# Leaving two products and the router in PSUM banks: a fused state-space, attention and expert kernel on one core

## The reference, cut to what matters

```python
def _ssm_layer(x, A_log, Dp, W_dbc, W_dt, b_dt):
    A = -jnp.exp(A_log)
    dbc = jnp.einsum('ble,ce->blc', x, W_dbc)
    delta, Bm, Cm = jnp.split(dbc, [DT_RANK, DT_RANK + N_STATE], axis=-1)
    delta = jax.nn.softplus(jnp.einsum('blr,er->ble', delta, W_dt) + b_dt)
    dA = jnp.exp(delta[..., None] * A)
    dBx = (delta * x)[..., None] * Bm[:, :, None, :]
    ...
    _, hs = jax.lax.associative_scan(combine, (dA, dBx), axis=1)
    y = jnp.einsum('blen,bln->ble', hs, Cm)
    return y + Dp * x
...
for i in range(NUM_LAYERS):
    x = _ssm_layer(x, A_log[i], D[i], W_dbc[i], W_dt[i], b_dt[i])
    if i < NUM_LAYERS - 1:
        ...
        x = x[:, :l // 2 * 2].reshape(b, l // 2, 2, d).mean(axis=2)
...
y = A * jnp.einsum('bhni,bhnj,bhije->bhne', qn, qn, kv_mod) + scale ** 2 * Bc * jnp.einsum('bhnd,bhde->bhne', qn, kv) + scale ** 4 * Cc * vsum
...
expert_logits = jax.nn.softmax(rh @ router_w2 + router_b2, axis=-1)
top_w, top_i = jax.lax.top_k(expert_logits, TOP_K)
routing_weights = jax.nn.softmax(top_w, axis=-1)
```

## Time and profile before

| | kernel before |
|---|---|
| runs, median (lowest to highest) | 741.2 us (737.34 to 743.2) |
| the profiled execution's span | 739.2 us |
| TensorE (PE) busy | 649.1 us, 88% |
| VectorE (DVE) busy | 569.2 us, 77% |
| ScalarE (ACT) busy | 519.2 us, 70% |
| GpSimd (POOL) busy | 361.2 us, 49% |
| chain that ended last, by engine | PE 46%, DVE 20%, ACT 14%, DMA 6%, issue 5%, SP queue 4%, POOL 2% |

### The profile page before, as it was taken

One profiled execution on the slowest core, in us unless ns is written; L12 is line 12 of the kernel. 1 busy time (PEld: TensorE's weight loads), 2 busy tenths in 40 slices (PEclk: granted clock), 3 DMA queues, 4 the chain that ended last, 5 costly groups with the idle time before them and its releaser, 6 DMA issues.

```text
span 739.2 us, 25719 instructions
## 1 busy us (share of the span) xinstructions
PE 649.1 (88%) x11131; PEld 375.6 (51%) x11131; DVE 569.2 (77%) x1078; ACT 519.2 (70%) x964; POOL 361.2 (49%) x317
## 2 busy tenths in 40 slices
PE   2667778989998899999989999898999999999983
PEld 2234445555546466545655465554565645555431
DVE  3879789988796799987698779885989986465451
ACT  1244358787868697778858787777887768878762
POOL 7444667757262727485355354472656563221010
PEclk9989899999999999999999999999999999999996
DMA  4332122122102111202112112221110100000001
GB/s 94 67 69 49 38 65 51 45 46 57 44 10 52 28 44 31 62 22 50 44 26 66 29 43 57 61 48 39 34 29 16 25 17 13 19 2 13 13 12 27
DMA packets 77596, 28.72 MB, mean 39 GB/s; under 512 B 69281, under 2 KB 77473, under 8 KB 77473
## 3 DMA queue, kind: packets, MB, share of 16 engines
q1 hardware_dynamic: 71300, 25.92, 15.4%
q10 hardware_dynamic: 6173, 1.05, 0.8%
HBM read 13.25 MB, written 3.05 MB: 22 GB/s over the span
## 4 chain that ended last, share of the span: by engine, by line
PE 46%; DVE 20%; ACT 14%; DMA 6%; issue 5%; SPq 4%; POOL 2%; ACTq 2%; POOLq 0%; DVEq 0%
PE ring L1244 9%; PE ring L1258 7%; PE ring L1346 5%; PE ring L1359 4%; ACT pm L1048 4%; DVE carry_A L1683 3%; PE ring L1425 2%; SPq L726 2%; PE ring L1231 2%; PE ring L1434 2%; PE ring L1211 2%; DVE hidw L1796 2%; DMA x_C<-x_C 1%; DMA x_B<-x_B 1%; PE ring L1454 1%
## 5 line engine op out<-in xcount | busy, mean ns | idle before, releaser
L1048 ACT ACTIVATE pm<-ring,two_col 93x744 f32<-93x744 f32 x128 | 106.6, 874 | 19.1 <-PE ring L1346 18.4
L908 POOL TENSOR_TENSOR q_exp<-qk,mask_q 128x1488 f32<-128x1488 f32 x16 | 44.3, 2771 | 37.1 <-DVE qk L1741 37.0
L1346 PE MATMUL ring<-q_exp,qk 32*93 32x372 f32 x512 | 56.1, 509 | 4.4 <-ACT yT L1055 0.7
L1796 DVE TENSOR_TENSOR hidw<-hid,ring 128x744 f32<-128x744 f32 x48 | 44.3, 923 | 15.7 <-PE ring L1415 8.1
L886 POOL TENSOR_TENSOR du_A<-delta_A,x_A 128x744 f32<-128x744 f32 x16 | 30.0, 1875 | 53.9 <-ACT delta_A L986 39.2
L1083 ACT ACTIVATE hid<-ring,b_col 128x372 f32<-128x372 f32 x96 | 49.3, 568 | 8.3 <-PE ring L1434 4.5
L1359 PE MATMUL ring<-pm,v 97*32 97x93 f32 x2048 | 53.1, 245 | 0.5 <-ACT pm L1048 0.4
L1090 ACT ACTIVATE hid<-ring,b_col 128x744 f32<-128x744 f32 x48 | 42.3, 881 | 15.1 <-PE ring L1425 10.8
L1359 PEld LDWEIGHTS ring<-pm,v 97*32 97x32 f32 x2048 | 42.1, 110 | 14.2 <-issue 4.9
L893 POOL TENSOR_TENSOR base_A<-base_A,carry_A 128x744 f32<-128x744 f32 x16 | 33.2, 2076 | 32.0 <-DVE carry_A L1695 27.9
L919 POOL CAST gate_part<-gate 93x144 bf16<-93x144 f32 x16 | 5.4, 336 | 83.4 <-DVE gate L1791 83.4
(11 more groups left out here) (349 smaller groups left out, 1839.7 us busy)
## 6 DMA issues: line engine op xcount, KB each, us to landing
xin_A<-in_x_dram SPq DMA_DIRECT2D x62, 93.0 KB
xin_B<-in_x_dram SPq DMA_DIRECT2D x62, 93.0 KB
x_A<-x_A SPq DMA_DIRECT2D x32, 93.0 KB, 2.3
x_B<-x_B SPq DMA_DIRECT2D x32, 93.0 KB, 2.9
x_C<-x_C SPq DMA_DIRECT2D x32, 93.0 KB, 2.2
out_dram<-osb SPq DMA_DIRECT2D x15, 186.0 KB
x_D<-x_D SPq DMA_DIRECT2D x32, 46.5 KB, 2.0
w<-in_L_ffn_expert_w_dram SPq DMA_DIRECT2D x6, 48.0 KB
```

The costliest lines, as they stand in the source:

```text
L1048: a.activation(pm[q % 2][h][0:TOUT].rearrange("m a j n -> m a (j n)"), out_of(f"att.s{q}{h}", g)[0:TOUT, :, 0:COLS], ACT.Square, bias=two_ ...
L1346: ins = mm(o[h][0:TOUT, b, 0:COLS], qk[r:r + 32, 1, q * TOUT:(q + 1) * TOUT], q_exp[r:r + 32, q].rearrange("p j n -> p (j n)"), start=True ...
L1796: tt(hidw[k][:], hid2[:], out_of(f"ffn.g_{k}", g)[:, :, 0:COLS], ALU.mult).then_inc(me, 1)
```

## The change

The product b * du is written in place over b in its two PSUM banks, and the scan reads it there, with dec from SBUF; operands and operations change places, so that the state is decay * state + b * du. For that the b job writes 744 neighbouring columns across two banks (the first half starts at column 512 - 372), and state 0 is taken out of the sum in `s` (row 0 of w_c0 is zero). The product s * du is written in place over s, and D * x is added to it from there. The router's four arrays stand in the bank of its logits at columns 0, 64, 128 and 192, one of the one-hot arrays excepted. So b's banks are now freed by `scan`, s's by `based`, the logits' bank by `gate`. The number of VectorE and TensorE steps stays as it is, but for one preparation step (`prep.back`, 13 small VectorE instructions in place of GpSimd's 9 on row_back). The SBUF tiles vin, lg, pr, key and one oh are gone. ORDER is new on every engine, and so are the banks.

```diff
         JOBS = {f"{u}.{j}": (2, f"dve {u}.{r}") for u in UNITS
-                for j, r in (("z", "quad"), ("b", "vin"), ("s", "base"), ("c", "carry"))}
+                for j, r in (("z", "quad"), ("b", "scan"), ("s", "based"), ("c", "carry"))}
...
-                 "ffn.rh": (2, "act ffn.rh"), "ffn.lg": (1, "dve ffn.route1"), "ffn.gT": (1, "act ffn.gateT"),
+                 "ffn.rh": (2, "act ffn.rh"), "ffn.lg": (1, "dve ffn.gate"), "ffn.gT": (1, "act ffn.gateT"),
...
+        def b_made(u, g):
+
+            return out_of(f"{u}.b", g).rearrange("p b c -> p (b c)")[:, 512 - WIDE[u]:512 + WIDE[u]]
+
+        def router(g, k):
+
+            n_at = 64 * ("lg", "pr", "key", "rsum").index(k)
+            o_ = out_of("ffn.lg", g)[0:TOUT, 0]
+            return o_[:, n_at:n_at + GB] if k == "rsum" else o_[:, n_at:n_at + GB * NX].rearrange("m (b e) -> m b e", e=NX)
...
-            spots = sem("spots")
-            for t_ in row_back.values():
-                g.memset(t_[:], 0.0).then_inc(spots, 1)
...
                 if s == "vin":
-                    o = made_by("b")
+                    need(g, f"pe {u}.b")
                     need(g, f"pool {u}.du")
-                    tt(halves(vin[u][:, 1:W + 1]), o, halves(du[u][:]), ALU.mult).then_inc(me, 1)
+                    tt(b_made(u, g), b_made(u, g), du[u][:], ALU.mult).then_inc(me, 1)
                 if s == "scan":
                     need(g, f"dve {u}.vin", f"act {u}.decay")
                     need(g, f"pool {u}.y", back=1)
-                    v.tensor_tensor_scan(carry[u][:], vin[u][:, 0:W], dec[u][:], 0.0, ALU.add, ALU.mult).then_inc(me, 1)
+                    v.tensor_tensor_scan(carry[u][:], dec[u][:], b_made(u, g), 0.0, ALU.mult, ALU.add).then_inc(me, 1)
                 if s == "base":
                     o = made_by("s")
                     need(g, f"pool {u}.du")
-                    need(g, f"pool {u}.{'y' if u == 'D' else 'pooled'}", back=1)
-                    tt(halves(base[u][:]), o, halves(du[u][:]), ALU.mult).then_inc(me, 1)
+                    tt(o, o, halves(du[u][:]), ALU.mult).then_inc(me, 1)
                 if s == "based":
                     need(g, f"dve {u}.base")
-                    stt(halves(base[u][:]), xs[u][:, 0::2, :], d_col[:, l:l + 1], halves(base[u][:]), ALU.mult, ALU.add).then_inc(me, 1)
+                    need(g, f"pool {u}.{'y' if u == 'D' else 'pooled'}", back=1)
+                    stt(halves(base[u][:]), xs[u][:, 0::2, :], d_col[:, l:l + 1], out_of(f"{u}.s", g)[:, :, 0:wide],
+                        ALU.mult, ALU.add).then_inc(me, 1)
```

In the table ORDER the first entries of the lists of act and sp read before and now:

```diff
-            "act": ("prep.l3:0 A.x:0 B.x:0 prep.exp:0 prep.l2:0 prep.l5:0 A.row:0 B.row:0 A.exp:0 A.ln:0 B.exp:0 ...
+            "act": ("prep.l5:0 B.x:0 prep.exp:0 A.x:0 B.row:0 A.row:0 B.exp:0 B.ln:0 A.exp:0 A.ln:0 A.decay:0 ...
-            "sp": ("prep.l4:0 prep.l1:0 A.load:0 B.load:0 A.swap:0 B.swap:0 prep.l0:0 B.load:1 A.load:1 ...
+            "sp": ("A.load:0 B.load:0 prep.l4:0 A.load:1 B.swap:0 A.swap:0 prep.l1:0 B.load:1 prep.l0:0 ...
```

More of the change, by code:

```diff
@@ L1654, in prepare @@
                     dve.wait_ge(c, 14)
-                k = ("w0", "w1", "w2", "dec", "mean", "qkvp", "late", "cen", "most", "mostof", "ends", "flags", "again").index(s)
+                k = ("w0", "w1", "w2", "dec", "mean", "qkvp", "late", "cen", "most", "mostof", "ends", "flags", "again", "back").index(s)
                 v.memset(tick[:, k:k + 1], 0.0).then_inc(me, 1)
@@ L1778, in experts @@
[L1778 to L1783 removed]
+                    step(v.tensor_reduce(st[:, 1], pr, AX_X, ALU.add), "sum")
```

103 lines of the change are left out of this document (54 added, 49 removed), and 654 rows, old and new, of the table ORDER.

## The result

The changed kernel takes 697.2 us (median, 696.2 to 699.5) where the kernel before takes 740.1 us beside it: a ratio of 0.942 (95% interval 0.938 to 0.946), 43 us less. The forecast was 724 us with a range of 704 to 741.

What follows compares the result with a forecast made beforehand. TensorE, 94% busy in the middle, was taken as the bound. 739.2 - 8 (start) - 7 (blocking) - 3 (order) + 3 (banks) = 724 us profiled, 726 as median, 2 us rounded in for the clock: 724 us, range 704 to 741.

Steps and rivals of the forecast that it cites:

- The scan's and addition's stopped time goes: VectorE's scans lose 12.6 us of time blocked by GpSimd, the D * x additions 8.1 us; together 20.7 of 569 us.
- I take 7 for the blocked time: Middle of the kernel: of TensorE's 36.9 idle us, 7 come back because VectorE and GpSimd no longer block each other.
- Start: 8 us: Kernel start: earlier rows and first scan give TensorE 5 us before 40 us and 3 us from 40 to 100.
- near 29: Kernel start: the first scan comes near 29 us instead of 41.57, 12 us earlier.
- rows_A's wait: Kernel start: ScalarE's rows_A waits until 25.82 us behind six b_col DMA issues, although its matmul ended at 21.9.
- And 3 for the evenness of the new order: Middle of the kernel: more evenly spaced row jobs of A and VectorE load give 3 us.
- +3 for the banks: TensorE's in-order queue: PSUM banks held longer make it wait for late readers, costing 3 us.
- The rival of the slower side: TensorE's queue in the middle: longer bank holds cost 25 us, giving 748 us; chance 0.11.
- The matmuls are the same. The time can therefore fall only by what those gaps give back: TensorE: with unchanged matmuls, only its idle gaps can shrink; 65.1 of 90.1 idle us are open.
- Writes into PSUM: VectorE's products and router steps writing to PSUM (272 instructions) were taken to cost zero extra.
- near 75 us: Sign in the new profile: TensorE's idle time near 75 us, 30 or less of it from 100 to 700.
- The rival at 708 us: TensorE's gaps close much further: half of the 65.1 us open goes, giving 708 us; chance 0.19.

Runs made afterwards that it cites:

- x5: Kernel before, maxima of one SBUF operand replacing scan and D * x addition, product with c reading vin, so GpSimd stops neither: 723.5 us, ratio 0.977.
- x9: Changed kernel with 64 more VectorE maxima over 186 columns, one ahead of each scan: 705.5 us, ratio 0.953.
- x14: x5 with 64 more VectorE maxima over 186 columns, spread ahead of the scans: 730.6 us, ratio 0.987.
- x7: Changed kernel with the late-weight DMA issues in ScalarE's list placed as before: 704.6 us, ratio 0.952.
- x6: Changed kernel with products in SBUF, maxima replacing scan and addition, b's and s's banks freed at the products, router kept in its bank: 698.0 us, ratio 0.943.
- x8: Kernel before with only the late-weight DMA issues placed as in the changed kernel: 754.0 us, ratio 1.017.
- x1: Changed kernel's order, banks and start, but both products and the router's arrays in SBUF as before: 765.4 us, ratio 1.037.
- x4: Changed kernel with the router's arrays back in SBUF and the logits' bank freed at the first router step: 716.8 us, ratio 0.970.
- x13: x5 with seven z jobs two or three places later in TensorE's list: 729.2 us, ratio 0.985.

## Why the prediction was wrong, step by step

- **"The scan's and addition's stopped time goes": right.** 12.6 us forecast and 11.9 measured for the scan (108.21 to 96.33), 8.1 and 4.8 for the addition (61.18 to 56.34). The addition's stopped time did go; the other 2.8 us did not, since it doesn't run at the product's rate from PSUM: 0.980 us, as from SBUF (0.987 in the earlier trace rows). GpSimd's pooling lost 12.4 us, as worked out.
- **"I take 7 for the blocked time": the term that was mis-sized, 17 us instead of 7** (x5). I took a third of VectorE's 20.7 us to arrive, since TensorE had work queued. Of these, 17.9 us were stopped time (12.6 and 61.2 - 55.9 = 5.3), and taking it away brought 17, nearly all of it. A third to a half is the rate of evenly spread time (x9, x14). Stopped time comes in pieces of up to 2.5 us and takes GpSimd's time along (361 to 324 us in x5).
- **"Start: 8 us": right in size.** x7 gives 7.4, and x6 leads x5 by 8 at the 1,000th matmul. The first scan came at 30.94 ("near 29"), x itself at 20.21 (18.1 forecast). The reason was half right, so the size is partly luck. The place of the issues is worth the 7 us in the new kernel only; in the old one rows_A's wait, which I had named, held nothing (x8). There TensorE's order of jobs was the bound, but not at the place that I named: the transposes of group 1 waited 0.6 us for their data before, while A.s, ahead of B's row job, waited 3.7 us for quad_A.
- **"And 3 for the evenness of the new order": the largest miss.** Without stopping, the new order is worth 25 us (x5 to x6), some 8 at the start and 17 behind it, where I had 3. I had read the order for its distances (A's row jobs, 56 to 69 jobs apart by the list from group 5 on) and given that a token price.
- **"+3 for the banks": not seen** (x6 shows no price for the holds, to within some 3 us; TensorE's waits on scans and additions come to 4 us). The rival of the slower side, the same mechanism at 25 us, falls with it. The Trainium skill (PSUM - Partial Sum Buffer, section Summary: rules for kernel authors) asks to evacuate PSUM promptly; here no run shows a price for holding these banks longer under the new order and its bank list.
- **"The matmuls are the same. The time can therefore fall only by what those gaps give back": false.** 15.3 of the 43.6 us came from a shorter busy time. Neither half brings it alone: TensorE is busy for 653.2 us in x1 and for 645.0 in x5, but for 633.0 in x6. Part is the granted clock (0.976 to 0.986 of 649 us is 6.6 us, an estimate). The rest isn't shown; I can only place it: jobs soon behind a gap can take longer. In the changed kernel's start, two jobs of one form, both at a granted clock of 1.00, the first of them 1.6 us behind the end of a gap of 1.92 us:

```profile
22.76 1.52 PE L1220 MATMUL ring<-rows_B,row_back_dpre 64*64 64x186 f32 x16
24.05 0.86 PE L1220 MATMUL ring<-rows_A,row_back_dpre 64*64 64x186 f32 x16
```

- **Writes into PSUM "zero": right.** 0.938 us against 0.926 in the earlier trace rows, and the router's shift 0.211 against 0.203: 0.01 us each. For reading from PSUM the Trainium skill (VectorE: DVE Perf Modes, section The TRN2 errata) would have had 65 ns more for each instruction, an estimate from its 58 and 120 cycles; the rows don't show it (scans and additions above, with one operand in PSUM). I had counted some 330 such instructions; by the code they are 352. The router was costed at nothing, as it was hardly stopped before. True for the old order; in the new one its PSUM arrays are worth 20 us (x4), a term that my sum doesn't have.
- **The whole.** The steps that failed are the 3 us for the new order (25 measured, with the start's 8 in them) and the 7 us for the blocked time (17). With the start's 8 these make up the 42 or 43 us measured. The sum was made part by part, each against the old state of the other. But the data flow is what makes the new order pay: 25 us of loss turn into 25 us of gain. TensorE's idle time, "near 75 us", is 61.8. The rival at 708 us ("the gaps close much further") named the direction, and its price, half of the open gaps, was still 11 us short.

What stays open is which property of the new order brings the 17 us behind the start. TensorE idles 13.8 us from 100 to 650 us in x6 and 22.6 in x5. More tolerance to VectorE's time isn't it (x14); the waits for the swaps aren't settled by x13, which brought new waits. Evenness of the load fits the rows and wasn't isolated: in the five stretches of 100 us from 100 to 600 us, VectorE is busy for 76 to 87 us in x5 and for 82 to 86 in x6.
